# Causal attention without a mask in the transposed scores: forbidden probabilities are zeroed by an integer product on GpSimd

## The reference

```
scores = jnp.einsum('bhsd,bhtd->bhst', qh, kh) * scale
mask = jnp.triu(jnp.ones((Sq, Sq), dtype=bool), k=0).at[0, 0].set(False)
scores = jnp.where(mask, -jnp.inf, scores)
probs = jax.nn.softmax(scores, axis=-1)
out = jnp.einsum('bhst,bhtd->bhsd', probs, vh)
```

## Time and profile before

| | |
|---|---|
| median of 3 runs | 1883.38 us |
| profiled execution, its own time | 1879.95 us |
| its span | 1877.0 us |
| TensorE busy | 1519.4 us (81%) |
| VectorE busy | 1393.7 us (74%) |
| ScalarE busy | 781.4 us (42%) |
| GpSimd busy | 511.7 us (27%) |
| mean granted clock of TensorE | 0.921 of full speed |

### The profile page before, as it was taken

The page is one execution under the profiler, slowest core; times in us unless marked ns, Lnnn a source line. Parts: engine busy times, 40 slices in busy tenths (PEclk is TensorE's granted clock), DMA queues, the critical chain, the costliest instruction groups (busy, mean ns, idle before and its releaser), DMA issues. The chain is left out here.

```text
span 1877.0 us, 33463 instructions
## 1 busy us (share of the span) xinstructions
PE 1519.4 (81%) x10824; PEld 925.0 (49%) x10824; DVE 1393.7 (74%) x3602; ACT 781.4 (42%) x1314; POOL 511.7 (27%) x559
## 2 busy tenths in 40 slices
PE   3888894488889799889889899935788899778787
PEld 1455552255555465555555455522355556445454
DVE  5777776667776547888887888876567667698997
ACT  1555563145556423334333333422356556333332
POOL 0000000000000003354353443553000000477786
PEclk9998897589999899999999999975999999899998
DMA  7444530254253000000000000004053532000000
GB/s 170 68 70 57 71 53 1 34 145 70 41 69 55 1 1 1 6 1 7 6 0 6 0 7 18 1 0 73 9 70 43 71 47 35 1 1 12 11 12 12
DMA packets 62833, 63.59 MB, mean 34 GB/s; under 512 B 6064, under 2 KB 57776, under 8 KB 62128
## 3 DMA queue, kind: packets, MB, share of 16 engines
q1 hardware_dynamic: 62704, 61.99, 20.3%
HBM read 22.12 MB, written 2.10 MB: 13 GB/s over the span
## 5 line engine op out<-in xcount | busy, mean ns | idle before, releaser
L1208 DVE TENSOR_REDUCE neg_max<-bank 128x4 f32<-128x512 f32 x384 | 260.4, 687 | 114.2 <-PE bank L839 108.0
L653 ACT ACTIVATE probs<-bank 128x512 f32<-128x512 f32 x384 | 229.2, 598 | 237.7 <-PE bank L862 235.3
L1009 PEld LDWEIGHTS bank<-room,area 128*128 128x128 f32 x2048 | 254.7, 199 | 100.2 <-issue 63.0
L439 POOL TENSOR_SCALAR rstd_a<-meanvar 128x4 f32<-128x4 f32 x64 | 17.0, 266 | 1023.5 <-DVE meanvar L1164 1023.5
L1009 PE MATMUL bank<-room,area 128*128 128x128 f32 x2048 | 264.0, 284 | 31.2 <-DVE area L1489 17.3
L729 ACT ACTIVATE work<-bank 128x512 f32<-128x512 f32 (+1 forms) x192 | 114.6, 597 | 358.0 <-PE bank L1034 353.1
L1038 PE MATMUL bank<-xT,room 128*128 128x512 f32 (+1 forms) x384 | 201.1, 606 | 16.2 <-DVE area L1489 16.1
L837 PE MATMUL bank<-mask_b,ident_b 128*128 128x512 bf16 x384 | 158.0, 412 | 66.7 <-DVE neg_max L1208 55.3
L1489 DVE TENSOR_TENSOR area<-work,bank 128x512 f32<-128x512 f32 (+1 forms) x192 | 128.8, 679 | 99.3 <-PE bank L1038 78.2
L1034 PE MATMUL bank<-xT,room 128*128 128x512 f32 (+1 forms) x384 | 198.3, 598 | 0.0
L551 POOL TENSOR_TENSOR prod<-mask_i,work 128x128 f32<-128x128 f32 (+3 forms) x128 | 126.6, 1022 | 156.7 <-DVE mask_i L1550 156.7
(11 more groups left out here) (164 smaller groups left out, 2402.6 us busy)
## 6 DMA issues: line engine op xcount, KB each, us to landing
q_rows<-area SPq DMA_DIRECT2D x144, 128.0 KB
k_rows<-area SPq DMA_DIRECT2D x288, 64.0 KB
ctxT<-ctx_t SPq DMA_DIRECT2D x24, 256.0 KB, 8.0
mask_i<-mask SPq DMA_DIRECT2D x8, 256.0 KB, 8.5
work<-ctx_in SPq DMA_DIRECT2D x8, 256.0 KB, 2.8
out<-x SPq DMA_DIRECT2D x4, 512.0 KB, 3.2
room<-w_down SPq DMA_DIRECT2D x1, 1536.0 KB, 13.8
room<-w_gate SPq DMA_DIRECT2D x1, 1408.0 KB, 6.3
```

Source lines behind the costliest of these rows:

```text
L653: act.activation(probs[j].rearrange("p a b -> p (a b)"), T_BANK[j % 2][:], ACT.Exp).then_inc(exp_done, 1)
L1009: mm = pe.matmul(dst[:, t * P:(t + 1) * P], h[:, t * P:(t + 1) * P], w, start=i == 0, stop=i == len(terms) - 1)
L1208: dve.tensor_reduce(neg_max[:, 4 * j:4 * j + 4], S_BANK[j % 2][:].rearrange("p (h k) -> p h k", h=4), AX.X, ALU.max, negate=True).then_inc ...
```

## The change

In attention 1 alone, `scores_t` no longer puts the mask matmul ahead of its four matmuls: each of them starts its own quarter of the bank. The exps thus also give values at forbidden places. GpSimd multiplies the bits of `probs[j]`, read as int32, by a constant int32 pattern of ones and zeros (`bound1`, 128x128, repeated over the four heads), in place, and counts `probs_masked`. `weigh` waits for `probs_masked` where it waited for `exp_done`. The mask in `scores`, from which the maxima come, stays. The pattern is loaded once, by a DMA of 64 KB that is queued behind the second x load. `inv_std` of a group now stands in GpSimd's stream behind the products 0 and 1 of the group's first tile and ahead of its products 2 and 3.

```diff
@@ -119,6 +119,7 @@
         ident_b = sb("ident_b", [P, P], BF16)
         strict = sb("strict", [P, P])
         mask1_b = sb("mask1_b", [P, P], BF16)
+        bound1 = sb("bound1", [P, P], I32)
         mask3_i = sb("mask3_i", [P, P], I32)
         mask3_b = sb("mask3_b", [P, P], BF16)
         wa = sb("wa", [P, 12, P])
...
@@ -323,6 +324,7 @@
             sp.dma_start(strict[:], consts_in[1]).then_inc(loaded, 16)
             sp.dma_start(wa[:], w_attn).then_inc(w_loaded, 16)
             load_x(1, 1, x_second)
+            sp.dma_start(bound1[:], allowed_in).then_inc(bound_loaded, 16)
 
             def load_rest():
                 sp.dma_start(rows[:], rows_in.partition_broadcast(P)).then_inc(rows_loaded, 16)
...
@@ -460,10 +462,22 @@
                 walk(pool, body, ch, 4)
 
             def attention(a):
+                def forbid(n, j):
+
+                    pool.wait_ge(exp_done, 4 * (N0[1] + n) + j + 1)
+                    pool.tensor_tensor(probs[j].bitcast(I32), probs[j].bitcast(I32), bcast(bound1[:], 4), ALU.mult).then_inc(probs_masked, 1)
+
                 def body(gp, first, last, a=a):
                     for gr, b, _, left in groups(gp, first, last):
-                        if left >= 2:
-                            inv_std(L0[a] + gr + 3)
+                        for t in range(TG if a == 1 else 1):
+                            for j in range(4 if a == 1 else 0):
+                                forbid(TG * gr + t, j)
+                                if j == 1 and t == 0 and left >= 2:
+                                    inv_std(L0[a] + gr + 3)
+                            if a != 1 and left >= 2:
+                                inv_std(L0[a] + gr + 3)
+                if a == 1:
+                    pool.wait_ge(bound_loaded, 16)
                 walk(pool, body, ch, 2)
 
             def feed_forward3():
...
@@ -855,17 +869,21 @@
                         pe.wait_ge(exp_done, 4 * (N0[a] + n) + j - 1)
                     dst = T_BANK[j % 2]
                     tok = slice(t * P, (t + 1) * P)
-                    pe.matmul(dst[:], mask(b, t), bcast(ident_b[:], 4), start=True, stop=False)
+                    if a != 1:
+                        pe.matmul(dst[:], mask(b, t), bcast(ident_b[:], 4), start=True, stop=False)
                     if j % 2 == 0:
                         pe.wait_ge(maxT_ready, 2 * (N0[a] + n) + j // 2 + 1)
                     for i in range(4):
                         mm = pe.matmul(dst[:, i * P:(i + 1) * P], k_rows[b][:, i % 2, 2 * j + i // 2, tok],
-                                       q_rows[b][:, 2 * j + i // 2, tok], start=False, stop=i == 3)
+                                       q_rows[b][:, 2 * j + i // 2, tok], start=a == 1, stop=a == 1 or i == 3)
                     mm.then_inc(t_filled, 1)
 
                 def weigh(n, b, t, j, v_count, a=a):
 
-                    pe.wait_ge(exp_done, 4 * (N0[a] + n) + j + 1)
+                    if a == 1:
+                        pe.wait_ge(probs_masked, 4 * n + j + 1)
+                    else:
+                        pe.wait_ge(exp_done, 4 * (N0[a] + n) + j + 1)
                     if j == 0:
                         if positive(N0[a] + n):
                             pe.wait_ge(heads_read, N0[a] + n)
...
@@ -1706,7 +1724,7 @@
         "w2": c(i["L2_ffn_w2"].T.reshape(4, P, P).transpose(1, 0, 2)),
         "gate3": c(i["L3_ffn_gate_w"].T), "mlp1": c(mlp1), "mlp2": c(i["L3_ffn_mlp2_w"].transpose(2, 0, 1)),
         "mlp2_b": mlp2_b, "cols_in": cols, "rows_in": rows, "consts_in": consts,
-        "pick_in": pick,
+        "pick_in": pick, "allowed_in": np.where(allowed.T, 1, 0).astype(np.int32),
     }
```

More of the change, by code:

```diff
@@ L105, in program @@
 def program(nc, x_in, ctx_in, ctx_t, mask0, mask3, w_attn, w_ffn0, w_router, w_gate, w_up, w_down, w1, w2, gate3,
-            mlp1, mlp2, mlp2_b, cols_in, rows_in, consts_in, pick_in, out):
+            mlp1, mlp2, mlp2_b, cols_in, rows_in, consts_in, pick_in, allowed_in, out):
     with ExitStack() as ctx:
@@ L223, in program @@
             tok_scored tok_products tok_probs tok_summed tok_shifted tok_exp tok_written w2_ready
-            h3_ready product_ready lin_taken x_first x_second rows_loaded lin_ready pick_loaded""".split()
+            h3_ready product_ready lin_taken x_first x_second rows_loaded lin_ready pick_loaded bound_loaded probs_masked""".split()
         (loaded, w_loaded, init_pool, init_dve, setup_act, setup_dve, x_loaded, x_written, stats_ready,
@@ L233, in program @@
          tok_products, tok_probs, tok_summed, tok_shifted, tok_exp, tok_written, w2_ready, h3_ready,
-         product_ready, lin_taken, x_first, x_second, rows_loaded, lin_ready, pick_loaded) = (sem(n) for n in names)
+         product_ready, lin_taken, x_first, x_second, rows_loaded, lin_ready, pick_loaded, bound_loaded, probs_masked) = (sem(n) for n in names)
         ctx_tok_loaded = [sem(f"ctx_tok_loaded{b}") for b in range(2)]
```

## The result

The changed kernel takes 1948.94 us, median of 4 runs (1944.62 to 1957.26), against 1885.37 us, median of 4 runs before: ratio 1.0351, 95% interval 1.0319 to 1.0383. It is slower by 64 us (by 66 in the spans of the profiled executions); 1966 was forecast. Ratios and intervals leave out one slow run, of the kernel with no mask and no product: it took 2916 us where its other nine took 1863 to 1874.

The account below looks back on a forecast made before the run. TensorE's in-order stream was taken to bound attention 1; product latency, held-up VectorE and statistics would add 67 us in six groups and 18 in the last tiles, +85 on 1879.95, forecast 1966 us, range 1922 to 2045.

Parts of the forecast that it names:

- TensorE's stream bounds the stage, nothing lies between exp and weigh: Attention 1 before: TensorE busy 6.04 of 6.09 us a plain tile; `weigh` 0 starts 0.18 us after its exp.
- Product 1.29 us, integer no dearer: Each 128x512 GpSimd product in attention 1 takes 1.29 us, as an ordinary f32 product; upper bound 2.58.
- Plain tile 8.0 by latency alone, 8.75 with VectorE held up: Attention 1 plain tile, 6.08 us before: 8.0 from waits for products, 8.75 with VectorE's operation ahead of `turn_max` held up.
- The 0.75 for L1250: Plain tile: VectorE's two-SBUF-input step of the maxima waits for GpSimd, taking the tile from 8.0 to 8.75 us.
- turn_max near 7.05: Plain tile: `turn_max` starts near 7.05 us after exp 0 starts, the maxima step getting through at 6.76.
- Three products in a row: Plain tile's loop: products 0, 2 and 3 stand one after the other, so the 0.88 us saved goes into stalls.
- Group 43.8: One of six groups in attention 1: intervals together 42.3 us plus 1.5 for TensorE's clock, against 32.65 before.
- Last eight tiles +18: End of attention 1, 49.69 us before: seven intervals +18.7, a covered stall -3.4, drain +2.6, together +18.
- Sum +85: Whole kernel: +67 us from six groups and +18 from the last tiles, on the profiled 1879.95, giving 1965.
- Rival without side effects: Attention 1: products do not hold VectorE up; plain tile 8.0, group 40.6, total 1940 us; chance 0.24.
- rival slow product: Attention 1: integer product takes 2.58 us and GpSimd bounds the tile at 12.4, total 2065 us; chance 0.16.
- rival hidden: Attention 1: products are hidden and the 28 us of mask time is a gain, total 1852 us; chance 0.05.

Follow-up runs that it names:

- c_one_part: Changed kernel with the second part of the maxima (L1250) in attention 1 a memset of zero; 1949.36 us, ratio 1.0356.
- l_off_path: Changed kernel with all 128 products written to a spare buffer and `weigh` waiting for exp alone, mask left out of the result; 1916.65 us, ratio 1.0195.
- a_no_product: Changed kernel with no product at all, so no mask in attention 1's transposed scores, `weigh` waiting for exp; 1871.8 us, ratio 0.9936.
- i_float: Changed kernel with float products in place of integer ones, overflowed exps not zeroed; 1960.7 us from 2 runs, ratio 1.0440.

## Why the prediction was right, and where it was not

- *TensorE's stream bounds the stage, nothing lies between exp and weigh.* Right: the wait for GpSimd is there, 1.28 us before `weigh 0` where I had 1.6. My hand-over from ScalarE to GpSimd was 0.18; it is 0.07 (671.30 to 671.37).
- *Product 1.29 us, integer no dearer.* Right: 1.267, and float 1.266. The estimate by the Trainium skill (GPSIMD Engine Reference, section "3. Performance versus the Vector engine"), bound by the read port, agrees in kind: an integer product is no dearer. Its 1.11 us before dispatch lies below the 1.267 of the trace.
- *Plain tile 8.0 by latency alone, 8.75 with VectorE held up.* 7.96. The first value fits by luck in part: the true tile has L1250 held up and shorter hand-overs. The 0.75 for L1250 was mis-sized: c_one_part shows 0.26. The step that failed is "turn_max near 7.05"; product 3 ended 6.41 us after the start of exp 0 (674.60 + 2.51 - 670.70) where I had 6.76, and `turn_max` came at 6.49. A second slip lies in the step behind it: the 1.68 from `turn_max` to exp 0 still holds the mask matmul of 0.22 that the change removes, and it measures 1.47 (669.23 to 670.70). These two make 0.77 of the 0.79.
- *Three products in a row.* Partly: the slope measured between half and full width is two, because the path over exp 3 ends as late as the one over product 2. The forecast had both at 5.47 and did not say that a shorter product would win only two.
- *Group 43.8.* Measured 258.12 / 6 = 43.0. Counted as the forecast does, from exp 0 to exp 0, groups 1 to 5 give for the first tile 13.5 to 15.3, 14.5 on average (12.8, and 14.3 with the clock's share, forecast); for the two with a projection 9.5 and 9.0 on average (9.64 each forecast); for the one with the splits 10.2 (10.25 forecast), with a subtraction of 2.17 us in it (timeline, VectorE):

```profile
591.57 2.17 DVE L1241 TENSOR_TENSOR area<-area 128x1024 f32<-128x1024 f32 x1
```

  That they come so near is luck in part: the plain tile under them is 0.79 shorter than forecast, and what I had missed altogether, that norm and casts with one SBUF input are held up too, makes up for part of it.
- *Last eight tiles +18.* They took 706.67 - 643.84 = 62.83 us, which is +13.1 (49.69). The stretch starts at the second tile of group 6, so it holds six intervals and the last tile, not seven intervals: the six, stall covered, gave +7.8, and the last tile with the drain +5.3, twice the 2.6 forecast.
- *Sum +85.* The stage is +76.9, the medians differ by 64. The term that was too large is the plain tile, 0.79 us too long, at the end and under the projection tiles of the groups: 18 - 13.1 = 4.9 at the end and 67 - 62.2 = 4.8 in the groups; the stretch ahead of the first tile, forecast unchanged, is 1.6 longer (385.72 - 349.96 against 391.24 - 357.08). What remains between 77 and 64 is spread between executions that I did not settle. The last step of the forecast has a slip too: 1965 and 3.4 are 1968, not 1966.
- *Rival without side effects (1940), rival slow product (2065), rival hidden (1852).* The first is denied by l_off_path against a_no_product, 52 us of stage with no product in front of `weigh`; its number lies nearer to the median than mine (9 us against 17), while of the stage it explains +60 and I had +85, of +76.9: latency and collisions overlap more than I had them. The second by i_float. The third by every run; a_no_product shows that even a free product would have given 1872, not 1852.

## What to carry to other kernels

An idle engine is not free work: count the latency of what you put there against the gap between producer and consumer (0.18 us here), and look at what its instructions hold up. Before moving work off the busiest engine, run the kernel with that work simply left out: here 28 us of TensorE time were worth 10, the most that any product on GpSimd could have earned. When a stall is removed by a new order of instructions, look where it comes back: the late statistics turned a wait of 4.49 us into two of 2.3.

## What the runs showed of the hardware

- While a GpSimd product with two SBUF inputs runs, VectorE's operations with two SBUF inputs wait for its end: 0.17 us became 1.20. So do some with one SBUF input, a norm (1.12 to 3.02 us for four) and a cast (174 to 491 ns on average with the products off the path). The score maximum, read from PSUM, does not wait (0.69 us throughout). The Trainium skill (Advanced Engine Details and Errata, section "VectorE Performance Modes") says that GpSimd and VectorE's two-port modes block each other, and lists casts and tensor_scalar, but not tensor_tensor, among what can run in them. The norm (a tensor_scalar) and the casts agree with it, though no run here shows their mode; that two-input operations wait is what the traces show beyond that section.
- A GpSimd memset, which only writes, leaves two-input operations alone (1225 and 292 ns, as without it) but still holds up the norm (911 against 343 ns) and the cast (956 against 683).
- It goes both ways: the longest product took 2247 ns beside a median of 1267. It started at 504.58 us while a subtraction of the splits ran from 503.53 to 505.70.
- GpSimd products of 128x256 and 128x512 take 725 and 1267 ns, so 256 more elements a partition cost 542 ns and the fixed part is about 183. Int32 and f32 take the same time.
